# A GINE layer on one core: x by rows moves to "node n in partition n / 56", pairs of blocks become m and m + 28

## The reference

```
msg  = relu(x[src] + edge_attr @ We + be)
aggr = segment_sum(msg, dst)
h    = relu(((1 + eps) * x + aggr) @ W1 + b1) @ W2 + b2
h    = (h - mean) * rsqrt(var + 1e-5) * gamma + beta      # over the nodes
r    = relu(h) + x
out  = layernorm(x + r)                                   # over the features
```

## Time and profile before

| what | value |
|---|---|
| median of 3 runs | 1559.09 us (1558.66 to 1559.86) |
| the profiled execution | 1564.18 us, span 1562.2 us |
| PE busy | 1416.0 us (91%) |
| ACT busy | 1255.7 us (80%) |
| POOL busy | 1160.5 us (74%) |
| DVE busy | 891.9 us (57%) |
| last piece of xb landed | 57.2 us after the span's start |
| first gather from xb | 57.9 us |

### The profile page before, as it was taken

The page is one execution under the profiler, slowest core; times in us unless marked ns, Lnnn a source line. Parts: engine busy times, 40 slices in busy tenths (PEclk is TensorE's granted clock), DMA queues, the critical chain, the costliest instruction groups (busy, mean ns, idle before and its releaser), DMA issues.

```text
span 1562.2 us, 60471 instructions
## 1 busy us (share of the span) xinstructions
PE 1416.0 (91%) x23435; PEld 1095.0 (70%) x23435; DVE 891.9 (57%) x3174; ACT 1255.7 (80%) x3729; POOL 1160.5 (74%) x1193
## 2 busy tenths in 40 slices
PE   1299999999999999989999999989999999999954
PEld 1277777777777777767777777767777777777734
DVE  5676665655566565555555556555556555655436
ACT  2488888888888888878877888878788888888845
POOL 7677777777777777777777777777777777777762
PEclk9999999999999999999999999999999999999967
DMA  9644445444544445444444444445444444444432
GB/s 250 170 111 109 109 113 123 113 111 117 119 113 110 108 112 126 109 106 113 111 108 106 113 106 113 112 106 117 108 110 107 111 112 107 105 112 110 104 125 84
DMA packets 148516, 180.72 MB, mean 116 GB/s; under 512 B 41725, under 2 KB 128980, under 8 KB 147972
## 3 DMA queue, kind: packets, MB, share of 16 engines
q1 hardware_dynamic: 102489, 89.62, 24.5%
q0 software_dynamic: 37728, 77.31, 20.9%
q10 hardware_dynamic: 8011, 9.90, 2.3%
HBM read 170.09 MB, written 6.63 MB: 113 GB/s over the span
## 4 chain that ended last, share of the span: by engine, by line
PE 55%; POOL 21%; issue 8%; ACT 5%; DVE 4%; DMA 4%; SPq 1%; ACTq 0%; POOLq 0%; DVEq 0%
POOL xg L590 21%; PE ps L1396 20%; PE ps L1381 14%; PE ps L1325 9%; PE ps L1311 6%; DMA xg<-xb,idxb 3%; ACT hot L747 2%; ACT msg L753 1%; PE ps L1362 1%; ACT hot L740 1%; PE ps L1342 1%; PE ps L1365 1%; PE ps L1334 1%; PE ps L1337 1%; SPq L480 1%
## 5 line engine op out<-in xcount | busy, mean ns | idle before, releaser
L590 POOL DMA_INDIRECT xg<-xb,idxb x1145 | 1107.0, 967 | 356.9 <-issue 337.0
L1396 PE MATMUL ps<-iota_all 128*128 128x128 bf16 x8064 | 518.0, 220 | 0.0
L1396 PEld LDWEIGHTS ps<-iota_all 128*128 128x128 bf16 x8064 | 452.3, 98 | 87.1 <-issue 67.7
L984 DVE TENSOR_TENSOR msg<-ps,xg 128x512 f32<-128x512 f32 x390 | 264.5, 688 | 305.6 <-DMA xg<-xb,idxb 192.8
L707 ACT ACTIVATE iota_all<-ps 128x384 bf16<-128x384 f32 x896 | 379.8, 484 | 31.7 <-PE ps L1381 28.4
L740 ACT ACTIVATE hot<-iota,rel 128x64 f32<-128x64 f32 x1560 | 391.6, 339 | 0.0
L1381 PE MATMUL ps<-x,iota_all 112*32 112x384 bf16 x7168 | 365.1, 331 | 0.0
L1069 DVE TENSOR_TENSOR accT<-accT,ps 128x64 f32 x390 | 86.2, 221 | 292.4 <-PE ps L1342 248.1
L753 ACT ACTIVATE msg<-msg 128x512 f32<-128x512 f32 x390 | 241.0, 618 | 14.7 <-DVE msg L984 14.7
L1381 PEld LDWEIGHTS ps<-x,iota_all 112*32 112x32 bf16 x7168 | 156.9, 96 | 120.6 <-issue 38.5
L1325 PE MATMUL ps<-msg,hot 128*64 128x128 f32 x3120 | 219.4, 284 | 23.1 <-ACT msg L753 23.1
(11 more groups left out here) (145 smaller groups left out, 800.3 us busy)
## 6 DMA issues: line engine op xcount, KB each, us to landing
ea<-in_eat SPq DMA_DIRECT2D x156, 320.0 KB
lowB<-lowD SPq DMA_DIRECT2D x128, 224.0 KB
xg<-xb,idxb POOLq DMA_INDIRECT x1145
accT<-in_xt ACTq DMA_DIRECT2D x1, 3125.0 KB, 14.8
x<-in_xt ACTq DMA_DIRECT2D x1, 3125.0 KB, 11.0
out<-iota_all SPq DMA_DIRECT2D x5, 512.0 KB
iota_all<-in_x ACTq DMA_DIRECT2D x3, 784.0 KB, 17.6
xb<-iota_all SPq DMA_DIRECT2D x3, 784.0 KB, 16.8
```

The source lines that it names most:

```text
L590: pool.indirect_dma_start(out=xg[0:rows, slot, j, :], out_offset=None, in_=of, in_offset=bass.IndirectOffsetOnAxis(ap=index, axis=0)).then ...
L984: add = dve.tensor_tensor(both, lin_of(half), xg[:, g % RING, :, :].rearrange("p (b t) h -> p b (t h)", b=2), ALU.add)
L1396: last = pe.matmul(found[:, e, :], sel2[set_of(k)][:, t, e * P:(e + 1) * P], rows3[:, t, a, :], start=(t == 0 and e == 0 and a == 0), stop ...
```

## The change

`xrow` and `x3` hold node n in partition n // 56, block n % 56. One partition's share of a piece is then 14 successive nodes, 7168 bytes that lie together in HBM and in SBUF. 6250 nodes fill 111 partitions, and the 112th (`LASTP` = 111) holds the remaining 34 (`LASTR`). A piece is moved by one DMA of 111 partitions, and where the last partition has nodes in it (pieces 0, 1 and 2) by a second DMA of that one partition. What is cleared ahead of the loads is the unused end of the last partition, in a rectangle that starts at partition 96. In `split_sources` and `pick` the pair of a source becomes src % 28 and the place in it src // 28.

```diff
+    LASTP = SUB - 1
+    LASTR = N - LASTP * NSUB
...
-            return 16 * (1 + (q == NQ - 1 and N % SUB > 0))
+            return 16 * (1 + (PIECES[q][0] < LASTR))
...
-                sp.dma_start(xb[a * SUB:whole * SUB, :].rearrange("(b p) h -> p b h", p=SUB), xrow[0:SUB, a:whole, :])\
+                sp.dma_start(xb[0:LASTP * NSUB, :].rearrange("(p b) h -> p b h", b=NSUB)[:, a:b, :], xrow[0:LASTP, a:b, :])\
                   .then_inc(s_xb[q], 16)
-                if whole < b:
-                    sp.dma_start(xb[whole * SUB:N, :], xrow[0:N - whole * SUB, whole, :]).then_inc(s_xb[q], 16)
+                if a < last:
+                    sp.dma_start(xb[LASTP * NSUB + a:LASTP * NSUB + last, :].rearrange("(p b) h -> p b h", p=1),
+                                 xrow[LASTP:SUB, a:last, :]).then_inc(s_xb[q], 16)
...
-                act.dma_start(xrow[0:SUB, a:whole, :], x[a * SUB:whole * SUB, :].rearrange("(b p) h -> p b h", p=SUB))\
+                act.dma_start(xrow[0:LASTP, a:b, :], x[0:LASTP * NSUB, :].rearrange("(p b) h -> p b h", b=NSUB)[:, a:b, :])\
                    .then_inc(s_xrow[q], 16)
...
-            step(dve.memset(xrow[:, NSUB - 1, :], 0.0))
+            step(dve.memset(xrow[LASTP // 32 * 32:SUB, LASTR:NSUB, :], 0.0))
...
-                dve.scalar_tensor_tensor(out=low_of.rearrange("p (m c) -> p m c", c=HALF), in0=part_of, scalar=-pair, in1=source,
-                                         op0=ALU.mult, op1=ALU.add)
-                step(dve.tensor_scalar(start_of.rearrange("p (m c) -> p m c", c=HALF), part_of, float(CAP), None, ALU.mult))
+                dve.tensor_copy(low_of.rearrange("p (m c) -> p m c", c=HALF), part_of)
+                step(dve.scalar_tensor_tensor(out=near, in0=part_of, scalar=-pair, in1=source, op0=ALU.mult, op1=ALU.add))
+                step(dve.tensor_scalar(start_of.rearrange("p (m c) -> p m c", c=HALF), near, float(CAP), None, ALU.mult))
...
-                    pe.wait_ge(s_rest[1], min(NQ, max(2, -(-2 * PAIRS * (t + 1) // PIECE))))
+                    pe.wait_ge(s_rest[1], min(NQ, -(-(NPAIR + PAIRS * (t + 1)) // PIECE)))
...
-                                         x3[0:SUB, 2 * m + u, :, :].rearrange("p a h -> p (a h)"),
+                                         x3[0:SUB, u * NPAIR + m, :, :].rearrange("p a h -> p (a h)"),
```

More of the change, by code:

```diff
@@ L81, in gine_layer_kernel @@
     NQ = len(PIECES)
+    LASTP = SUB - 1
+    LASTR = N - LASTP * NSUB
+    assert 0 < LASTR <= NSUB
     SORTED = (2, 5, 8, 11, 14, 17, 20, 23, 26, 29)
@@ L498, in keep_lifted @@
                 a, b = PIECES[q][0], sum(PIECES[q])
-                whole = min(b, N // SUB)
+                last = min(b, LASTR)
                 sp.wait_ge(s_lifted, q + 1)
-                sp.dma_start(xb[a * SUB:whole * SUB, :].rearrange("(b p) h -> p b h", p=SUB), xrow[0:SUB, a:whole, :])\
+                sp.dma_start(xb[0:LASTP * NSUB, :].rearrange("(p b) h -> p b h", b=NSUB)[:, a:b, :], xrow[0:LASTP, a:b, :])\
                   .then_inc(s_xb[q], 16)
-                if whole < b:
-                    sp.dma_start(xb[whole * SUB:N, :], xrow[0:N - whole * SUB, whole, :]).then_inc(s_xb[q], 16)
+                if a < last:
+                    sp.dma_start(xb[LASTP * NSUB + a:LASTP * NSUB + last, :].rearrange("(p b) h -> p b h", p=1),
+                                 xrow[LASTP:SUB, a:last, :]).then_inc(s_xb[q], 16)
             def spread_lows(j, k):
@@ L655, in _ @@
                 a, b = PIECES[q][0], sum(PIECES[q])
-                whole = min(b, N // SUB)
-                act.dma_start(xrow[0:SUB, a:whole, :], x[a * SUB:whole * SUB, :].rearrange("(b p) h -> p b h", p=SUB))\
+                last = min(b, LASTR)
+                act.dma_start(xrow[0:LASTP, a:b, :], x[0:LASTP * NSUB, :].rearrange("(p b) h -> p b h", b=NSUB)[:, a:b, :])\
                    .then_inc(s_xrow[q], 16)
-                if whole < b:
-                    act.dma_start(xrow[0:N - whole * SUB, whole, :], x[whole * SUB:N, :]).then_inc(s_xrow[q], 16)
+                if a < last:
+                    act.dma_start(xrow[LASTP:SUB, a:last, :],
+                                  x[LASTP * NSUB + a:LASTP * NSUB + last, :].rearrange("(p b) h -> p b h", p=1))\
+                       .then_inc(s_xrow[q], 16)
             act.dma_start(accT[:, 0:N], xt).then_inc(s_xt, 16)
@@ L954, in constants @@
                 dve.tensor_scalar(starts[:, :], iota[:, 0:NPAIR], float(CAP), None, ALU.mult)
-                dve.tensor_copy(nodeu[:, 0:1], nodes[:, 0:1])
-                dve.tensor_scalar(nodeu[:, 1:2], nodes[:, 0:1], float(SUB), None, ALU.add)
+                dve.tensor_scalar(nodeu[:, 0:1], nodes[:, 0:1], 2.0, None, ALU.mult)
+                dve.tensor_scalar(nodeu[:, 1:2], nodes[:, 0:1], 2.0, 1.0, ALU.mult, ALU.add)
             def split_sources():
                 dve.wait_ge(s_srcT, 1)
-                pair = 2.0 * SUB
+                pair = float(NPAIR)
                 source = ps[:, 3:7, :].rearrange("p a n -> p (a n)")[:, 0:LOOPED * GROUP]\
                     .rearrange("p (m c) -> p m c", c=CYCLE)[:, :, CYCLE - HALF:CYCLE]
-                step(dve.tensor_scalar(near, source, 0.5 - SUB, 1.0 / pair, ALU.add, ALU.mult))
+                step(dve.tensor_scalar(near, source, 0.5 - pair / 2, 1.0 / pair, ALU.add, ALU.mult))
                 step(dve.tensor_scalar_add(part_of, near, 12582912.0))
                 step(dve.tensor_scalar_add(part_of, part_of, -12582912.0))
-                dve.scalar_tensor_tensor(out=low_of.rearrange("p (m c) -> p m c", c=HALF), in0=part_of, scalar=-pair, in1=source,
-                                         op0=ALU.mult, op1=ALU.add)
-                step(dve.tensor_scalar(start_of.rearrange("p (m c) -> p m c", c=HALF), part_of, float(CAP), None, ALU.mult))
+                dve.tensor_copy(low_of.rearrange("p (m c) -> p m c", c=HALF), part_of)
+                step(dve.scalar_tensor_tensor(out=near, in0=part_of, scalar=-pair, in1=source, op0=ALU.mult, op1=ALU.add))
+                step(dve.tensor_scalar(start_of.rearrange("p (m c) -> p m c", c=HALF), near, float(CAP), None, ALU.mult))
             dve.nop().then_inc(s_tr, 1)
```

## The result

| | us |
|---|---|
| before, median (4 runs, 1557.72 to 1559.86) | 1558.88 |
| changed kernel, median (4 runs, 1615.10 to 1615.74) | 1615.26 |
| ratio, 95% interval | 1.0363 [1.0345, 1.0380] |
| forecast | 1610 (1595 to 1632) |

What follows compares the result with a forecast made beforehand. The DMA-bound start-up was taken to release POOL's unbroken gathers when xb lands. Three engines' 2.5 + 82.2 + 20.6 + 1.3 + 1.5 us move the landing from 57.2 to 108.1, so 1559.1 + 51 = 1610 us (1595 to 1632).

Steps and rivals of the forecast that it cites:

- How many engines: Loads of x, stores of xb: a DMA uses the largest number up to 16 dividing its rows; 111 rows use three.
- The rate: Loads and stores in 7168-byte runs: 25.8 GB/s an engine, 77.4 GB/s on three engines.
- The sum: Start-up on three engines: 2.5 + 82.2 + 20.6 + 1.3 + 1.5 us; last store of xb lands at 108.1, not 57.2.
- Nothing hides it: Behind the landing of xb: POOL goes without a break, so the landing's +51 us reaches the end whole.
- POOL's unbroken stream sets the end: After xb lands: POOL issues 1145 gathers without a break, 1.27 us apiece, leaving no room to win back a late start.
- Longer runs are worth almost a factor of two for each engine.: DMA start-up: 13.4 GB/s an engine loading x at 12 to 27 us, 25.8 with x transposed's long runs at 31 to 35.
- Spread over 16: Rival on x and xb DMAs: all 16 engines used anyway, landing at 40 to 45 us, time 1545; 4%.
- Pass each other: Rival on x and xb DMAs: an engine moves loads and stores both at full rate, landing near 78, +21, 1580; 5%.
- 7 KB no faster than short ones: Rival on x and xb DMAs: long runs gain nothing per engine; +84 us, 1643, or +127, 1686; 6%.
- It does nothing: Rival on the whole kernel: start-up is hidden elsewhere, time stays at 1559; 2%.
- The other edits: Memset (3.7 us, at most 0.2 felt), one more DVE cast (0.36 to 0.56 us), pick's waits, ACT's queue: cost nothing while landing is late.
- The signs: Profile after: DMA share 0.2 to 0.4, first xb gather about 109, POOL idle about 57 us before it, first pick near 120.

Runs made afterwards that it cites:

- e1: Changed kernel with each 111-partition DMA, loads and stores, cut in 96 and 15 partitions: 1558.24 us, 1.0003 to the kernel before.
- e3: Kernel before (old layout, 512-byte runs) with each 112-partition DMA of x and xb cut in 111 and 1: 1629.52 us, ratio 1.0453.
- e4: Changed kernel with UNBIASED 15 in place of 10, so POOL gathers groups 10 to 14 from x before its wait for xb: 1616.94 us, 1.0379.
- e7: e6 with the two first loads of edge attributes also issued behind all stores of xb: 1560.69 us, 1.0012 to the kernel before.
- run 22: Not a follow-up run: the words mean run length, 22 GB/s an engine with 512-byte runs in e3 against 26 with 7168-byte runs.
- e10: e1 with each piece of x loaded as 128 partitions of 6216 bytes (wrong values, same work behind it): 1556.41 us, one run, no ratio.
- e9: e1 with accT's load issued only after all of xb landed and first edge attributes behind the first lowD and lowB: 1557.07 us, 0.9969 to before.
- e12: Kernel before, old layout and 512-byte runs, with the reordering of e9 alone: 1555.90 us, ratio 0.9969.
- e2: Changed kernel with only the loads of x cut in 96 and 15 partitions, stores of xb kept at 111: 1586.06 us, 1.0176 to before.
- e11: Changed kernel with only the stores of xb cut in 96 and 15 partitions, loads kept at 111: 1591.25 us, 1.0178 to before.
- e8: Kernel before, old layout and 512-byte runs, with the two moves of e7: 1558.82 us, ratio 1.0002.
- e5: e1 with the sources of xrow and accT exchanged, copy shapes kept (wrong values, same work): 1557.77 us, one run, no ratio.
- e6: e1 with accT's load issued behind ACT's four first casts, not ahead of them: 1558.19 us, 1.0003 to the kernel before.

## Why the prediction was right, point by point

- *How many engines.* Right: 111 rows, three engines, by the 77 GB/s and the 2144 packets of the changed kernel, and by e1 and e3 (2256 and 8014 packets). The reading of the 106-row store and of the 15 closing packets of the 90 rows carried the case. "The largest number up to 16 that divides the count of rows" fits the counts of all these runs: 16 for 64, 96, 112 and 128 rows, 15 for 90 and 15 rows, 3 for 111, 2 for 106, 14 and 13 for the single partitions of 14 and 13 runs in e3, 1 for a single run. It is the author's reading of these counts; no other count of rows was run.
- *The rate.* Right for this kernel: 25.7 GB/s an engine measured, 25.8 taken.
- *The sum.* Landing forecast at 108.1, measured 113.7; this term is 5.6 us short, and the time with it (1610 for 1615.26). I had taken the other traffic at the rate of long runs, 20.6 us an engine, with its short packets and the gaps left out, though the bound of 30 us stood beside it. How the 5.6 us divide among the two is not settled.
- *Nothing hides it.* Right: of +56.5 us at the first `pick`, 56.4 arrive at the end.
- *POOL's unbroken stream sets the end.* Only half right. The stream is unbroken, but by e4 and e7 its release by xb alone is not what counts. It stands in a ring of 15 groups, and the later of POOL's own gathers and DVE's first message, behind the first `pick`, is what the time follows. The two were so close in the kernel before that its trace shows a wait at either, 6.4 and 1.9 us; the prediction didn't name the second. Both hang on the same landing, so the +51 us came out the same by either.
- *"Longer runs are worth almost a factor of two for each engine."* Wrong. The two stretches of the earlier trace rows differ in the run, and also in the partitions written (112 and 128) and the step between them. e3 gives the run 22 against 26 GB/s; e1 and e10, which differ in partitions and step, run at 215 and 383. The 25.8 for 7 KB runs came from this reading, and that it held was luck: three engines stay far under 215 in all, so the slow loads never showed.
- *The rivals.* "Spread over 16" was priced at 1545; e1 is that kernel, and measured 1558.24. Its loads were no faster (215 GB/s in all, as before), and accT's load was beside the stores. The price was too low by the prediction's own rows, too: POOL's wait of 6.4 us leaves no less than 1559.1 - 6.4 = 1552.7 as long as POOL's stream sets the end. e9, e10 and e12 gain 5.4 to 6.3 us. "Pass each other" fell with e2 and e11, whose halves add up. "7 KB no faster than short ones" was priced at 1643 with 512-byte rates; e3 with true short runs is 1629.52. "It does nothing" fell with the result.
- *The other edits.* No cost to be seen: e1 holds them all, and its ratio is 1.0003. The clearing of 16 partitions of 2816 numbers took 2.40 us in the changed kernel, for which the prediction had 3.7 at most.
- *The signs.* The first gather from xb came at 114.5 (109 forecast), the first `pick` at 125.7 (120), and POOL waited 67.7 us (57). The DMA share was 0.2 while only stores moved, as forecast, and 0.91 from 47 to 65 us, when accT's load ran on all engines.

## What to carry to other kernels

Before a DMA's shape is changed, factor its count of rows: 112 used 16 engines here, 111 used three, and nothing in the code's bytes or run lengths says so. Two stretches of a trace that differ in rate differ in more than one thing, and a single run with the other thing changed costs less than a wrong rule. When a landing is moved, ask what else waits behind the same data, and look at the last of them, which need not be the one with the longest wait; a few KB behind a megabyte in the same queue can be that last one (lowD in e7: 1.8 KB, 14.17 us to its landing).

## What the runs showed of the hardware

- The queue with the longer packets took the larger part of the engines: 25000-byte packets against 7168-byte and 1024-byte ones, 1.98 to 0.69 MB in 8 us (e7).
- The issue of accT's load took long where the loads ahead of it ran on three engines. In the changed kernel ACT's queue took 21.44 us to issue the load of accT, although the other 13 engines were little in use (DMA share 0.34, 5.4 engines of 16, from 24 to 46 us). In e11, with the loads on three engines as well, it took 14.21 us; in the kernel before 0.61, and in e1 and e2 0.41. The row of ACT's queue and the stretch:

```profile
24.25 21.44 ACTq L667 DMA_DIRECT2D accT<-in_xt  x1
```

```profile
24.00:46.00 22.00, 2.71 (x12) 2.31 (x12) 6.88 (x14) 0.00 (x0) 17.12 (x17) 1.00 0.34 115
```

- Loads that write 112 partitions, or 96 and 15, ran at 215 to 233 GB/s in all from 12 to 22 us, whether in runs of 512 bytes (before 215, e8 224, e12 215) or 7168 (e1 215, e5 220, e6 233, e7 219, e9 225); the loads of x that write 128 partitions in runs of 6216 bytes ran at 383 (e10, 12 to 18 us).
- Closing packets, by the counts of ACT's and SP's queue: 16 for a DMA of 64, 96, 112 or 128 rows, 15 for 90 or 15 rows, 3 for 111, 2 for 106 (before 8011 and 102489, and 34 packets under 512 bytes from 1558 us on; changed kernel 2144 and 96622; e1 2256 and 96734; e3 8014 and 102492; e10 2258 on ACT's queue).
